# C rows one state ahead in the state-space phase, and a reordered double tick in cross attention

## The reference, cut to what matters

```python
# layer 0, state-space block; 16 states per channel
h  = norm(x) @ w_in.T + b_in                 # h0 = h
hc = silu(norm(conv3(h) + conv_b))
Bm, Cm = hc @ w_B.T + b_B, hc @ w_C.T + b_C  # 16 columns each
Delta  = softplus((hc @ w_d1.T + b_d1) @ w_d2.T + b_d2)
state[l] = exp(-Delta*A) * state[l-1] + Delta * hc * Bm     # per state n, per channel
y = sum_n state_n * Cm_n + D * hc
out = norm(y * silu(h0)) @ w_out.T + b_out + x
# layer 0, cross attention; 16 heads of 64
scores  = Q K^T / 8 ; weights = softmax(scores) ; attn = weights V ; out = attn @ Wo.T + bo
```

## Time and profile before

| | us |
|---|---|
| median of 3 runs | 3709.29 |
| lowest, highest | 3705.96, 3709.39 |
| the profiled execution | 3702.01 |
| its span, first to last instruction | 3700.3 |

### The profile page before, as it was taken

One profiled execution on the slowest core, in us unless ns is written; L12 is line 12 of the kernel. 1 busy time (PEld: TensorE's weight loads), 2 busy tenths in 40 slices (PEclk: granted clock), 3 DMA queues, 4 the chain that ended last, 5 costly groups with the idle time before them and its releaser, 6 DMA issues. The chain is left out here.

```text
span 3700.3 us, 44165 instructions
## 1 busy us (share of the span) xinstructions
PE 3169.0 (86%) x12438; PEld 1675.1 (45%) x12438; DVE 1799.3 (49%) x2639; ACT 1979.0 (53%) x3736; POOL 1151.5 (31%) x954
## 2 busy tenths in 40 slices
PE   3777777769999999996667999999999769999997
PEld 1222222236777777763223444444444534444443
DVE  3877777754555555556994433433333321111110
ACT  3555555525555555553555777777777433323322
POOL 2666666631222222224663333333333000000000
PEclk9888888879999999998888999999999989999999
DMA  5333333320000000000110000000000210000001
GB/s 205 112 109 108 108 108 108 108 64 17 16 20 15 20 15 20 15 16 29 51 43 26 13 17 13 13 17 13 17 13 12 105 72 17 17 20 23 17 17 60
DMA packets 100808, 167.55 MB, mean 45 GB/s; under 512 B 11520, under 2 KB 42384, under 8 KB 100240
## 3 DMA queue, kind: packets, MB, share of 16 engines
q1 hardware_dynamic: 100752, 166.88, 13.4%
HBM read 81.57 MB, written 4.72 MB: 23 GB/s over the span
## 5 line engine op out<-in xcount | busy, mean ns | idle before, releaser
L1359 POOL TENSOR_TENSOR d_pr<-d_pr,d_keep 128x512 f32<-128x512 f32 x256 | 320.1, 1271 | 564.9 <-ACT d_pr L1517 564.9
L282 PE MATMUL a_py<-a_prod,consts 128*128 128x512 f32 x512 | 308.6, 693 | 78.8 <-DVE a_prod L535 46.2
L776 POOL TENSOR_TENSOR b_pn<-b_e,b_inv 128x616 f32<-128x616 f32 x128 | 161.3, 1260 | 671.7 <-DVE b_inv L955 671.7
L262 POOL TENSOR_TENSOR a_bx<-a_bcopy,a_drive_u 128x512 f32<-128x512 f32 x256 | 320.3, 1265 | 55.0 <-DVE a_state L529 54.6
L529 DVE TENSOR_TENSOR_SCAN a_state<-a_decay,a_bx 128x512 f32<-128x512 f32 x256 | 310.8, 1214 | 1.4 <-POOL a_bx L262 1.4
L882 ACT ACTIVATE b_yy<-b_py,y_bias 128x154 f32<-128x154 f32 x512 | 169.8, 385 | 248.0 <-PE b_py L822 247.8
L458 ACT ACTIVATE a_decay<-a_delta,neg_a 128x508 f32<-128x508 f32 x256 | 174.9, 684 | 177.0 <-DVE a_state L529 175.5
L1912 PE MATMUL f_ph<-f_hb,wb 128*128 128x512 f32 x512 | 232.8, 599 | 6.3 <-ACT f_hb L1947 6.3
L1912 PE MATMUL f_ph<-f_ha,wb 128*128 128x512 f32 x512 | 229.0, 596 | 2.3 <-DVE f_ha L1976 2.3
L535 DVE TENSOR_TENSOR a_prod<-a_state,a_pc 128x512 f32<-128x512 f32 x256 | 175.8, 687 | 101.6 <-issue 90.5
L282 PEld LDWEIGHTS a_py<-a_prod,consts 128*128 128x128 f32 x512 | 102.3, 219 | 219.4 <-DVE a_prod L535 124.0
(11 more groups left out here) (282 smaller groups left out, 6535.0 us busy)
## 6 DMA issues: line engine op xcount, KB each, us to landing
a_bcopy<-rows SPq DMA_DIRECT2D x256, 256.0 KB, 3.3
wb<-in_wb SPq DMA_DIRECT2D x1, 6714.0 KB, 33.5
x<-in_x SPq DMA_DIRECT2D x1, 4096.0 KB
a_xf<-x SPq DMA_DIRECT2D x16, 256.0 KB, 3.8
a_xt<-x SPq DMA_DIRECT2D x16, 256.0 KB, 2.3
x<-a_xo SPq DMA_DIRECT2D x16, 256.0 KB, 3.7
b_xf<-x SPq DMA_DIRECT2D x32, 128.0 KB, 2.0
b_xt<-x SPq DMA_DIRECT2D x32, 128.0 KB, 2.0
```

What stands on the lines that cost most here:

```text
L262: gp.tensor_tensor(bx[:, k % 4, :], bcopy[:, k % 4, :], drive_u[:, p, :], ALU.mult).then_inc(*bxt.step("bx"))
L282: mm(py[:], S["ident"][:], prod[:, j % 4, :], start=j == 0, stop=j == SLOTS - 1).then_inc(*pey.step("y"))
L1359: gp.tensor_tensor(half, half, keep[:].unsqueeze(1).to_broadcast([128, QP, SEQ]), ALU.mult).then_inc(*gmt.step(f"m{odd}"))
```

## The change

Nothing is computed otherwise; instructions are moved, a tile is replaced and waits move with them.

1. PE in the state-space phase: the spread of C lags by 1 slot instead of 2, so it runs one state ahead of DVE, and it stands first in every slot, ahead of the sum of products.
2. The front's stages 12 (its matmuls and drains), 13, 14 and 15 become 13, 14, 15 and 16, one slot later on PE, ACT, DVE and POOL; `lead` allows stages 16 and 17. On PE `bc` and `z` so stand behind the tail's `out` instead of ahead of it.
3. The clip writes into the PSUM bank `a_pf` instead of `a_f3`, ACT reads it there, and PE waits for that read (`e2`) before `z` overwrites the bank.
4. Cross attention: on PE a tick is now scores, keys, (projection in tick 2), weighted, keys, v, (variance in tick 2), turned. On ACT the copy of `b_pt_sb` is made at the start of the next tick (lag 2) instead of behind exp. On DVE the add of the bias stands behind the subtraction, and the residual, the square and the variance move from tick 3 to tick 2.

```diff
@@ ssm: lead
-            if k < SLOTS - LEAD:
-                if front:
-                    stage(k + LEAD, g + 1, 1 - p)
-            elif not isinstance(g, int) or g + 2 < G:
+            if front:
+                stage(k + LEAD, g + 1, 1 - p)
+            if k >= SLOTS - LEAD and (not isinstance(g, int) or g + 2 < G):
                 stage(k + LEAD - SLOTS, g + 2, p)
@@ ssm: PE, a slot
-                        if k != 4:
-                            sum_y(g, p, k, main, tail)
-                        if main:
-                            r = SLOTS * g + k
-                            if k == 0:
-                                pe.wait_ge(*gf.at("lo", g))
-                        if u := unit(g, p, k, 2, main, tail):
+                        if main and k == 0:
+                            pe.wait_ge(*gf.at("lo", g))
+                        if u := unit(g, p, k, 1, main, tail):
...
                             mm(pc[j % 2][:], S["sel"][:, STATES + j, :], bc3[:, pu, :], start=True, stop=True
                                ).then_inc(*pec.step("c"))
-                        if k == 4:
-                            sum_y(g, p, k, main, tail)
+                        sum_y(g, p, k, main, tail)
...
-                    if k == 12:
+                    if k == 13:
                         pe.wait_ge(*gf.at("silu", g))
+                        pe.wait_ge(*sf.at("e2", g))
                         pe.wait_ge(*sf.at("conv", g))
@@ ssm: ACT
-                        A(sig[:], f3[:], ACT.Exp, scale=-1.0).then_inc(*sf.step("e2"))
+                        A(sig[:], pf[:], ACT.Exp, scale=-1.0).then_inc(*sf.step("e2"))
...
-                    if k == 12:
+                    if k == 13:
                         act.wait_ge(*pef.at("bc", g))
...
-                    if k == 13:
+                    if k == 14:
                         act.wait_ge(*pef.at("z", g))
@@ ssm: DVE
                     if k == 10:
+                        V.tensor_scalar(b4(pf[:]), h0, -40.0, None, ALU.max).then_inc(*vf.step("clip"))
+                    if k == 14:
+                        dve.wait_ge(*sf.at("absz", g))
                         if begun(g - 1):
                             dve.wait_ge(*gf.at("delta", g - 1))
-                        V.tensor_scalar(b4(f3[:]), h0, -40.0, None, ALU.max).then_inc(*vf.step("clip"))
-                    if k == 13:
-                        dve.wait_ge(*sf.at("absz", g))
                         V.tensor_scalar(f3[:], pf[:], S["b_delta"], 0.0, ALU.add, ALU.max
@@ cross: PE, a tick
-                        if u := unit(g, p, d, 2, main, tail):
-                            weighted(*u)
                         if u := unit(g, p, d, 0, main, tail):
                             scores(*u)
...
-                        if u := unit(g, p, d, 1, main, tail):
-                            turned(*u)
+                        if u := unit(g, p, d, 2, main, tail):
+                            weighted(*u)
...
                         if tail and d == 2:
+                            pe.wait_ge(*so.at("sq", g - 1))
+                            mm(pout[:, N:2 * N], S["mean"], t2[:], start=True, stop=True).then_inc(*peo.step("var"))
+                        if u := unit(g, p, d, 1, main, tail):
+                            turned(*u)
@@ cross: ACT, a tick
+                        if u := unit(g, p, d, 2, main, tail):
+                            _, _, j, r = u
+                            act.wait_ge(*pet.at("t", r))
+                            if begun(r - 1):
+                                act.wait_ge(*pea.at("a", r - 1))
+                            for i in range(2):
+                                op = A(pt_sb[:, i, :], ptr[i][0:CTX, :], ACT.Copy)
+                            op.then_inc(*pcopy.step("p"))
                         if front:
                             keys(g + 1, q, 2 * d)
...
-                        if u := unit(g, p, d, 1, main, tail):
-                            _, _, j, r = u
-                            act.wait_ge(*pet.at("t", r))
...
-                            op.then_inc(*pcopy.step("p"))
+                        if tail and d == 2:
+                            act.wait_ge(*vo.at("sum", g - 1))
+                            A(t2[:], t1[:], ACT.Square).then_inc(*so.step("sq"))
```

57 lines of the change are left out of this document (25 added, 32 removed).

## The result

The changed kernel takes 3570.07 us (median of 4 runs, 3567.98 to 3576.01), the kernel before beside it 3707.87. The ratio is 0.9631, interval 0.9615 to 0.9648: 138 us less. The forecast was 3581 in a range of 3560 to 3640, with the likeliest case's own bounds at 3560 to 3610. The profiled execution took 3576.01 with a span of 3574.3, 126.0 less than the span before. The granted TensorE clock is 0.952 on average, as against 0.947.

A forecast was written before the change was run, and what follows sets the result against it. DVE bounds the state-space phase and PE cross attention, both with named stalls. Gains of 69.5 and 59 make 128 us off the profiled 3702.0, so 3574, and 3581 for a median; range 3560 to 3640.

The forecast's parts named there:

- the likeliest case: Whole kernel: the forecast itself, 128 us off for a median of 3581, given 55%.
- Slot 6: State-space, product's 1.16 us stall: becomes a wait for the convolution's drain; 0.15 gained 14 times, 2 us.
- The clip: State-space slot 8 on DVE: writing to PSUM takes 0.72 us, bounds 0.42 and 1.43; 10.5 us gained.
- Slots 11 and 12: State-space: a 3.4 us stall at relu(z) replaces slot 11's and relu's stalls over 14 groups; 27.2 us gained.
- the rival on the clock: State-space slot 11: PE's gaps still bring half clock, 51 us of the gain go, 3632; chance 19%.
- the forecast's own signs: State-space: right if groups are 41 to 42 us, clock near 1; wrong if relu idles over 5, two group lengths.
- Group 0 and slot 15: State-space: group 0 adds some 0.5 us; slot 15's product stalls of 2.02 go, 28.2 us gained.
- The state-space sum: State-space phase, all terms together: 2 + 10.5 + 27.2 + 1.6 + 28.2 = 69.5 us gained.
- the term of 59: Cross attention: groups of 24.7 instead of 26.43, 51 us over 30 groups, plus 8 in the last group.
- the same ring: Cross attention: scores, maximum and subtraction, exp, copy, `weighted`, scores again; waiting ticks take 5.96 to 6.07 us, others 5.09.
- second ring: Cross attention: late keys, late copy and variance wait form another ring, 25 us of gain lost, 3607; chance 15%.
- the other two: Whole kernel: the change doesn't do what it says, 3670, 5%; state-space PE at half clock makes it slower, 3755, 4%.

The follow-up runs named there:

- e12: The changed kernel with the clip back in SBUF and one extra unused fp32 matmul on PE in each of slots 9 and 10: 3576.80 us.
- e7: The changed kernel with one extra unused fp32 matmul on PE in each of slots 9 and 10: 3564.23 us.
- e6: The changed kernel with the clip back in the SBUF tile, ACT reading it there and PE not waiting for that read: 3599.04 us.
- e1: The kernel before with the state-space parts 1 to 3 of the change alone: 3637.42 us against 3706.41.
- e2: The kernel before with the cross-attention part 4 of the change alone: 3635.0 us against 3704.99.
- e11: The changed kernel with cross attention's variance matmul moved behind the scores of tick 3 and ACT's square to the end of tick 2: 3558.72 us.
- e9: The changed kernel with slot 11's row of C moved on PE behind the sum and `out`, ahead of `bc` and `z`: 3543.4 us.
- e9b: The changed kernel with the row of C behind the sum and `out` in slot 11, and behind the sum and convolution in slot 5: 3533.56 us.

## Why the prediction was right, point by point

**The bound.** DVE in the state-space phase and PE in cross attention, with their stalls as named. Right: removing exactly these stalls moved the time, and the parts added up to 139 of 138, well within their noise.

**Slot 6.** Said: the stall changes its name, 0.15 of 1.16 is gained, and the convolution's sum waits about 1. The sum waits 0.93. Over 15 groups the product's 17.4 became 14.3 there (24.3 less the first group's 10.0): 3 us, said 2. This was the step where one would have booked 17.

**The clip.** Said 0.72 and 10.5 us; measured 0.686, and 10.8 of DVE's time. e12 against e7 gives 12.6. In e6 the SBUF clip starts at 348.20 while POOL works from 348.08 to 349.35, and ends at 349.62, 0.27 after POOL:

```profile
348.08 1.27 POOL L261 TENSOR_TENSOR a_bx<-a_bcopy,a_drive_u 128x512 f32<-128x512 f32 x1
348.20 1.42 DVE L494 TENSOR_SCALAR a_f<-a_hpad 128x512 f32<-128x512 f32 x1
```

In the changed kernel POOL's instruction at 338.05 covers the whole clip at 338.17, and the clip takes 0.69. The Trainium skill, page SBUF — State Buffer, section "SBUF: two separate sides", calls the port pair that DVE and GpSimd share an exclusive lock, under which the loser waits for the other's whole instruction; with that rule the trace of e6 agrees, and by its 0.69 beside POOL's instruction the clip into PSUM does not wait for it.

**Slots 11 and 12.** Said: relu waits 3.4 in 14 groups, 74.8 - 47.6 = 27.2. Measured: 3.50 in most groups (the mechanism and its times fit to a tenth: `bc` said 366.5 for its end counted from a product's end at 362.6, so 3.9 later; here 343.16 to 347.04), but 5.2 or 4.9 in four. The 14 waits make 55.2 and the term 19.6: 7.6 short. Some 6.5 of them are the rival on the clock, in 4 groups of 14 and at 1.7 each instead of 3.7, because the clock comes back within `out` (1.91 for the sum and 1.85 for the first `out` matmul, 1.02 for the second, for `bc` and for `z`); the rest is the 3.50 where 3.4 was said. By the forecast's own signs both pictures are there: 41.4 between groups and a clock of 1.00 in ten groups, and in three of the other four relu idle for over 5 us (4.93 in the fourth) and a group of a second length, 43.1. I had said that no gap in the new order is as long as the one that brought the fall in the earlier trace rows, which is true, and taken from it that the clock would hold, which isn't.

**Group 0 and slot 15.** Group 0 gained its 1.9 in slot 11 but relu there waits 2.75, so some 0.9 lost where 0.5 was booked as gained. Slot 15's 28.2 are gone in full, at half clock, as said.

**The state-space sum.** Said 69.5, measured 69.0. This closeness is partly luck. DVE's groups by line of the changed kernel account for 89.5 (product) + 10.8 (clip) - 25.9 (relu) - 14.2 (convolution's sum) = 60.2, and the shortfall against 69.5 is the term of slots 11 and 12. But these rows are of one execution, the slowest of the four. The same rows of e1 give 89.7 + 10.8 - 22.9 - 14.5, and 1.3 less at the last `a_xo`: 64.4. There only three groups are long, and relu waits 1.53 in group 0 instead of 2.75. The profiled execution of e1 is 65.5 shorter than that of the kernel before, so the rows hold nearly all of it; the other 3.5 of the 69.0 are the spread between executions. The 4.4 ahead of the first `a_xo` in e1 are part of these rows. They aren't seen in the changed kernel (146.0 against 146.5), since relu's two waits ahead of that mark are 2.75 and 4.93 there and 1.53 and 3.24 in e1, and the first group starts a microsecond later. The 3.9 behind the last `a_xo` were in no term of mine.

**Cross attention.** The step that was mis-sized is the term of 59; e2 measured 70 (67.2 between the profiled executions). Three pieces, from the starts of the projections. The last three of the changed kernel:

```profile
1521.06 3.62 PE L844 MATMUL b_pout<-b_attn,wb 128*128 128x256 f32 x16
...
1541.79 3.62 PE L844 MATMUL b_pout<-b_attn,wb 128*128 128x256 f32 x16
...
1560.76 6.62 PE L844 MATMUL b_pout<-b_attn,wb 128*128 128x256 f32 x16 [0.79 <-DVE b_attn L938]
```

and of the kernel before, whose first one starts at 880.12 (814.54 in the changed kernel) and which comes to its last two so:

```profile
1646.42 3.62 PE L866 MATMUL b_pout<-b_attn,wb 128*128 128x256 f32 x16
...
1672.53 3.62 PE L866 MATMUL b_pout<-b_attn,wb 128*128 128x256 f32 x16
...
1688.64 5.41 PE L866 MATMUL b_pout<-b_attn,wb 128*128 128x256 f32 x16 [0.79 <-DVE b_attn L937]
```

The middle: groups of 24.36 and not 24.7, since a tick is 5.04 and not 5.09 (the transposes take 0.88 to the next piece instead of 0.93; scores and keys together take 1.65 and took 1.66); 29 x 2.06 = 60 where 51 was said for 30. The end: in the last group with scores a tick without keys and v is down to 3.3 (`weighted` 1535.11 to 1538.42), and the distance of its projection fell from 26.1 to 20.7, but the next one rose from 16.1 to 19.0, at a lower clock (the projection takes 6.62 instead of 5.41): 2.5 instead of the 8 booked. In e2, where that projection takes 3.72, the two are 20.7 and 17.95: 3.5. The start: the first projection comes 5.2 earlier in e2 (874.96 against 880.12), since the first group's ticks wait for the same ring; I had no term for it. These make 67.5 to 68.5. The variance's wait, said 0.33, is 0.31 (e11).

**The rivals.** No second ring. One of its signs is there, PE's weight load idle before the second keys (0.17 each, 20.2 us in all), but it costs nothing, since the tick is 5.04. The clock fell in part. Nothing spoke for the other two.

## What to carry over

A row that runs one state ahead with two buffers has to wait for the newest product, so whatever stands behind it on its engine inherits that wait. Put the long work that nobody holds up ahead of the waiting instruction in just those slots where it is due (e9 and e9b: 37 us, with only the place of one matmul changed). And when a stall is taken away on the bounding engine, look first at what the next instruction there waits for: of 89.5 us of stalls removed by the lead alone, 59 came back under other names.

## What was not expected of the hardware

The granted clock can fall with the same work ahead of it. PE was busy 2.60 of 5 us ahead of slot 11 in both kinds of group, with gaps of at most 1.2 us between its pieces there, and came to `out` at either level. Yet it wasn't by chance from group to group: in the changed kernel every fourth group was long, 167.3 us apart. In e1 and e11, whose state-space phase is the same, three groups were long and not four (relu at 263.70, 431.07 and 598.41 in e1), at nearly the same distance. No run here shows what sets this distance. Under these conditions a small change elsewhere, 0.7 us on DVE, cost 14 to 16 us through the clock, and two unused matmuls a group gave back 22. An ablation that moves DVE by a little is there best made twice, with and without such extra matmuls, or its number holds the clock's share too.
